# Edge layers of a graph network: TensorE's part of the running maxima ahead of the sum by node

## The chip, the cores and the metric

One core of one Trainium2 chip runs the kernel. The metric is the device time of one execution in microseconds; it is the median of three runs.

## What is computed

The reference is a graph network of four layers on 3,125 nodes with 128 features each and 103,125 edges, sorted by the node that they go to (`dst`). Each layer works on a normalized copy of the features and is added back to them. Layer 0 is a transformer convolution (two heads of 128, with 32 attributes per edge, and a small network behind it), layer 1 three graph attention convolutions in a row (four heads of 64, 64 and 32), layer 2 spline networks and an attention of the second kind (gatv2), layer 3 attention by dot products. Six times in all the same is done by edge; for a graph attention convolution it reads:

```
xp = (x @ W).reshape(n, H, C)
al_src = (xp * a_src).sum(-1)
al_dst = (xp * a_dst).sum(-1)
e = jax.nn.leaky_relu(al_src[s] + al_dst[d], NEG_SLOPE)
m = jax.ops.segment_max(e, d, num_segments=n)
p = jnp.exp(e - m[d])
denom = jax.ops.segment_sum(p, d, num_segments=n)
alpha = p / denom[d]
out = jax.ops.segment_sum(alpha[:, :, None] * xp[s], d, num_segments=n)
```

So each edge layer has a gather of rows by source, a maximum over the edges of each node, and a sum of weighted rows over the edges of each node.

## The kernel before

The function `message_pass` (L394) is called once for each of the six edge layers: kind conv (once), gat (three times), gatv2 and dot. Its edges lie in 427 groups of 256, two tiles of 128 edges each, so that a group's edges all go to nodes of one block of 128. Twelve groups are a chunk (the last three chunks have 7, 6 and 6), which makes 37 chunks. The gathered rows lie in a ring of three chunks. Everything is written out without loops on the chip.

The work goes through the chunks in steps (`steps`): in step i every engine reads chunk i (`expand`), takes the maxima of chunk i-1 (`node_maxima`, in gatv2 `all_maximum`), and sums chunk i-2 (`scatter`), group by group. The engines meet by semaphores:

- POOL (GpSimd) issues two indirect gathers per group (L476) into the ring. From the fourth chunk on it first waits for `scat` of the group three chunks back (L472), since its gathers write over that group's rows.
- PE (TensorE): `expand` (L786) spreads the block's node values to the edges by a matmul with a one-hot matrix (L795 gat, L802 dot and gatv2, L809 conv). `scatter` (L812) adds up the messages of a group by node with two matmuls (L820, x4 in the trace where a product of float32 is two passes) and raises `scat`; it waits for the one-hot matrix, the messages and a free bank. `node_maxima` (L823) makes one link of the maxima's chain in groups 0, 2, 4, 6 and 8: transposes at L833 (group 0), L837 and L838 (group 2), L842 and L843 (group 4), L848 (group 6), and the matmul L852 (group 8). `all_maximum` (L855) has two links, at groups 0 and 2.
- DVE (VectorE) makes the other links in groups 1, 3, 5, 7 and 9, each from what PE's link of the group before left in PSUM (`mx_ps`): scans over the edges L676 and L677; scans over the tiles L682 and L684; L689 to L693; the subtractions L699 to L701; L707 and L708. Beside it DVE weighs the rows of a group (`messages`, L609), adds a group's sums to the nodes' (`add`, L618, two groups behind the scatter), scales the sums of a block that goes on in the next chunk (L633), and in conv computes the logits (L553) and the one-hot matrices.
- ACT (ScalarE) makes one-hot matrices (L893 to L918), conv's messages (L929, which wait for the scatter of the group before), the exponentials (L949, L960) at group 9 and the shrink factor (L969) at group 11.
- SP issues the small loads.

The order of PE's work is that of the function `step` below: in the gat layers a group is scatter, maxima, expand; in the others expand of the next group, scatter, maxima.

Of the kernel before, what the change touches and what calls it, by code (L numbers as in the profile page):

```python
# [39 lines left out]
RING = 3  # L40
# [93 lines left out]
def behind(eng, sem, value):  # L134

    if not (isinstance(value, int) and value <= 0):
        eng.wait_ge(sem, value)
# [256 lines left out]
def message_pass(c, T, name, kind, H, C, W, F, table, nd, acc, attr=None, att=None, ring=None, own_to=None):  # L394
# [68 lines left out]
    with nc.Block() as block:  # L463
# [319 lines left out]
        def _(pe):  # L783
            def expand(i, r, g, use):

                n = BASE[i] + g  # L786
                block_of = pe.value_load(T.blk[0:1, bass.ds(n, 1)], min_val=0, max_val=NB - 1)
                mine = nd[:, bass.ds(block_of, 1), :].rearrange("p o w -> p (o w)")
                pe.wait_ge(s("ohT"), n + 1)
                pe.nop(nofuse=True)  # L790
                if gat:
                    for u in range(2):
                        t = 2 * g + u
                        at = t % 12 * 24
                        last = pe.matmul(ex_ps[:, t // 12, at:at + 24], ohT[:, n % OHB, u, :], mine, start=True, stop=True)  # L795
                    last.then_inc(s("ex"), 1)
                if dot or gatv2:
                    behind(pe, s("prod" if dot else "z"), n - EXB + 1)
                    pe.nop(nofuse=True)
                    width = P if dot else F  # L800
                    for u in range(2):
                        last = pe.matmul(ex_ps[:, n % EXB, u * width:(u + 1) * width], ohT[:, n % OHB, u, :],  # L802
                                         mine[:, 0:width], start=True, stop=True)
                    last.then_inc(s("ex"), 1)
                if conv:
                    for u in range(2):
                        behind(pe, s("logits"), 2 * n - 3 + u)
                        pe.nop(nofuse=True)
                        pe.matmul(ex_ps[:, 2 * (n % 2) + u, 0:F], ohT[:, n % OHB, u, :], mine, start=True, stop=True  # L809
                                  ).then_inc(s("ex"), 1)  # L810

            def scatter(i, r, g):  # L812
                m = BASE[i] + g
                pe.wait_ge(s("oh"), m + 1)
                pe.wait_ge(s("msg"), m + 1)
                pe.wait_ge(s("added"), m + 1)
                pe.nop(nofuse=True)
                for u in range(2):
                    rows = msgs[:, m % 2, u, :] if conv else ring[:, r, 2 * g + u, W - F:W]
                    last = pe.matmul(sc_ps[:, m % SCB, 0:F], oh[:, m % 4, u, :], rows, start=(u == 0), stop=(u == 1))  # L820
                last.then_inc(s("scat"), 1)

            def node_maxima(ch, r, at):  # L823
                if at == 0:
                    if conv:
                        pe.wait_ge(s("logits"), 2 * BASE[ch + 1])
                        if ch >= FULL:
                            pe.wait_ge(s("short"), ch - FULL + 1)
                    else:
                        pe.wait_ge(s("by_v"), ch + 1)  # L830
                    behind(pe, s("shrink_log"), ch)
                    pe.nop(nofuse=True)
                    pe.transpose(mx_ps[0:HT, V_T:V_T + P], lg[:, r if conv else 0, :], T.ident[:]).then_inc(s("v_T"), 1)  # L833
                if at == 2:
                    pe.wait_ge(s("ends"), 2 * ch + 2)
                    pe.nop(nofuse=True)
                    pe.transpose(row_of(0), fwd[:, P - 1:P], T.turn[0:HT, 0:HT])  # L837
                    pe.transpose(row_of(1), bwd[:, 0:1], T.ident[0:HT, 0:HT]).then_inc(s("rows_T"), 1)  # L838
                if at == 4:
                    pe.wait_ge(s("runs"), 2 * ch + 2)  # L840
                    pe.nop(nofuse=True)
                    pe.transpose(mx_ps[0:HT, INTO:INTO + 1], runs[:, 0, 0:HT], T.ident[0:1, 0:1])  # L842
                    pe.transpose(mx_ps[0:HT, INTO + 1:INTO + 2], runs[:, 1, 1:HT + 1], T.ident[0:1, 0:1]  # L843
                                 ).then_inc(s("into_T"), 1)
                if at == 6:
                    pe.wait_ge(s("whole"), ch + 1)
                    pe.nop(nofuse=True)
                    pe.transpose(mx_ps[:, WHOLE:WHOLE + HT], whole[:], T.ident[0:HT, 0:HT]).then_inc(s("whole_T"), 1)  # L848
                if at == 8:
                    pe.wait_ge(s("delta"), ch + 1)  # L850
                    pe.nop(nofuse=True)
                    pe.matmul(mx_ps[:, DELTA:DELTA + H], T.ones[:], delta[:], start=True, stop=True  # L852
                              ).then_inc(s("delta_all"), 1)

            def all_maximum(ch, at):  # L855
                if at == 0:
                    pe.wait_ge(s("by_v"), ch + 1)
                    pe.nop(nofuse=True)
                    pe.transpose(mx_ps[0:1, 0:P], top1[:], T.ident[:]).then_inc(s("v_T"), 1)
                if at == 2:  # L860
                    pe.wait_ge(s("delta"), ch + 1)
                    pe.nop(nofuse=True)
                    pe.matmul(mx_ps[:, P:P + 2], T.ones[:], delta[:], start=True, stop=True).then_inc(s("delta_all"), 1)

            def step(i, r, use, reads, maxima, sums_, before):
                read = SIZES[i] if reads else 0
                summed = SIZES[i - 2] if sums_ else 0
                if reads and not gat:
                    expand(i, r, 0, use)
                for g in range(GC):  # L870
                    if not gat and g + 1 < read:
                        expand(i, r, g + 1, use)
                    if g < summed:
                        scatter(i - 2, (r + 1) % RING, g)
                    if maxima:
                        if gatv2:
                            all_maximum(i - 1, g)
                        else:
                            node_maxima(i - 1, (r - 1) % RING, g)
                    if gat and g < read:  # L880
                        expand(i, r, g, use)

            steps(pe, step)

        @block.scalar
# [1165 lines left out]
```

## Time and profile before

| | |
|---|---|
| Median of 3 runs | 9,028.36 us (9,025.22 to 9,031.15) |
| The profiled execution | 9,009.74 us, span 9,007.9 |
| Busy share of the span | ScalarE 59%, TensorE matmuls 57%, GpSimd 57%, VectorE 51% |
| Granted TensorE clock, mean | 0.707 of full speed |
| Share of the 16 DMA engines | software queue 22.8%, hardware queue 8.1% |

The profile takes one execution. A group's idle time is what its engine stood before it, with the engine whose signal ended the wait; "issue" is time in which it waited for nothing that the profile shows, and "remote" is a signal without a sender in the trace. Where an engine that has long been done is named (a transfer of the first layer in a later one), the length is right and the name is not.

### The profile page before, as it was taken

Reading aid. Unit: us, or ns where it says so; the run is one execution under the profiler, and the core shown is the slowest. Engines: PE = TensorE matmul, PEld = TensorE weight load, DVE = VectorE, ACT = ScalarE, POOL = GpSimd, SP = SyncE. Lnnn points to the kernel's source line nnn. Section 1 sums busy time; section 2 is a strip of 40 time slices with the busy share of each in tenths; the row PEclk is TensorE's granted clock in tenths of the full one; section 3 lists DMA queues with packets and bytes.
Section 4 is the critical chain, followed back from the end, with each engine's and each line's share of the span. In section 5 each row is a group of like instructions: output and inputs, shape, how many; then the busy total and the mean of one; then the engine's idle time right before and its main releaser. Section 6 shows DMA issues by size and latency. Waiting matters only on the chain. (4 is left out here: it accounts for less than half of the span.)

```text
span 9007.9 us, 129245 instructions
## 1 busy us (share of the span) xinstructions
PE 5135.4 (57%) x21094; PEld 3892.3 (43%) x21094; DVE 4622.3 (51%) x15579; ACT 5326.5 (59%) x14791; POOL 5155.8 (57%) x5195
## 2 busy tenths in 40 slices
PE   4778877445555635555534444444565564566666
PEld 2444444334334424344423334433555553455555
DVE  3666666435444524444533333364565565455555
ACT  1777776256666546666636666663566664566665
POOL 3555553266666456666556666635666663566664
PEclk7999999667777767776755555566766766666666
DMA  2222221134434234444322222201222222333332
GB/s 67 72 74 74 71 74 51 52 105 112 110 111 111 86 110 111 113 111 112 102 70 69 70 68 70 66 15 47 67 66 66 66 66 67 97 107 108 108 110 78
DMA packets 428332, 744.58 MB, mean 83 GB/s; under 512 B 207788, under 2 KB 248113, under 8 KB 427439
## 3 DMA queue, kind: packets, MB, share of 16 engines
q0 software_dynamic: 205312, 519.10, 22.8%
q1 hardware_dynamic: 218976, 215.57, 8.1%
q8 instruction: 246, 4.03, 0.2%
q14 instruction: 518, 4.24, 0.2%
q10 hardware_dynamic: 3280, 1.64, 0.1%
HBM read 718.36 MB, written 17.56 MB: 82 GB/s over the span
## 5 line engine op out<-in xcount | busy, mean ns | idle before, releaser
L476 POOL DMA_INDIRECT gat_ring<-tab,gat_ixb x2562 | 2535.1, 989 | 1478.1 <-issue 792.4
L820 PE MATMUL gat_sc_ps<-gat_ring,gat_oh 128*128 128x264 f32 (+1 forms) x5124 | 1892.5, 517 | 1554.3 <-issue 775.4
L820 PEld LDWEIGHTS gat_sc_ps<-gat_ring,gat_oh 128*128 128x128 f32 x5124 | 1208.5, 281 | 1729.3 <-issue 1601.2
L912 ACT ACTIVATE gat_ohT<-gat_offT,one 128x256 bf16<-128x256 bf16 x1281 | 637.9, 498 | 1122.1 <-issue 935.6
L476 POOL DMA_INDIRECT conv_ring<-tab,conv_ixb x854 | 811.9, 951 | 674.0 <-issue 310.3
L476 POOL DMA_INDIRECT dot_ring<-tab,dot_ixb x854 | 833.3, 976 | 624.7 <-issue 306.8
L476 POOL DMA_INDIRECT gatv_ring<-tab,gatv_ixb x854 | 835.2, 978 | 517.7 <-issue 267.1
L898 ACT ACTIVATE gat_off<-iota,rel 128x128 bf16<-128x128 f32 x2562 | 867.9, 386 | 0.1
L618 DVE TENSOR_TENSOR acc<-acc,gat_sc_ps 128x264 f32 (+1 forms) x1281 | 486.6, 380 | 595.6 <-remote 297.3
L809 PE MATMUL conv_ex_ps<-nd,conv_ohT 128*128 x1708 | 602.8, 477 | 324.5 <-issue 111.7
L609 DVE TENSOR_TENSOR gat_ring<-gat_ring,gat_p_sb 128x520 f32<-128x520 f32 (+1 forms) x1281 | 767.2, 599 | 4.1
L929 ACT ACTIVATE conv_msgs<-conv_ring,conv_p_sb 128x161 f32<-128x161 f32 x1708 | 589.2, 416 | 287.7 <-remote 132.6
L820 PE MATMUL dot_sc_ps<-dot_ring,dot_oh 128*128 128x132 f32 x1708 | 446.2, 409 | 433.3 <-issue 371.7
L820 PE MATMUL gatv_sc_ps<-gatv_ring,gatv_oh 128*128 128x132 f32 x1708 | 416.8, 388 | 446.7 <-issue 317.8
L918 ACT ACTIVATE gat_oh<-gat_off,one 128x256 f32<-128x256 bf16 x1281 | 631.8, 493 | 32.4 <-PE gat_sc_ps L820 9.1
L893 ACT ACTIVATE gat_offT<-gat_rel_row,pid 128x256 bf16<-128x256 bf16 x1281 | 631.6, 493 | 8.3 <-DMA gat_rel_row<-d_rel 8.2
L553 DVE SCALAR_TENSOR_TENSOR conv_junk<-conv_ring,conv_ex_ps 128x161 f32<-128x161 f32 x1708 | 453.6, 317 | 344.5 <-PE conv_ex_ps L809 199.1
L820 PEld LDWEIGHTS dot_sc_ps<-dot_ring,dot_oh 128*128 128x128 f32 x1708 | 365.2, 295 | 486.1 <-issue 485.1
L820 PE MATMUL conv_sc_ps<-conv_msgs,conv_oh 128*128 128x322 f32 x1708 | 554.6, 450 | 16.9 <-issue 9.6
L820 PEld LDWEIGHTS gatv_sc_ps<-gatv_ring,gatv_oh 128*128 128x128 f32 x1708 | 342.8, 279 | 498.7 <-issue 495.3
L795 PEld LDWEIGHTS gat_ex_ps<-nd,gat_ohT 128*128 128x128 bf16 x2562 | 281.2, 123 | 641.1 <-issue 559.6
L809 PEld LDWEIGHTS conv_ex_ps<-nd,conv_ohT 128*128 128x128 f32 x1708 | 305.6, 198 | 543.7 <-issue 473.5
(455 smaller groups left out, 10073.3 us busy)
## 6 DMA issues: line engine op xcount, KB each, us to landing
gat_rel_row<-d_rel SPq DMA_DIRECT2D x216, 384.0 KB
gat_ring<-tab,gat_ixb POOLq DMA_INDIRECT x2562
conv_rel_row<-d_rel SPq DMA_DIRECT2D x72, 384.0 KB
gatv_rel_row<-d_rel SPq DMA_DIRECT2D x72, 384.0 KB
dot_rel_row<-d_rel SPq DMA_DIRECT2D x72, 384.0 KB
conv_ring<-tab,conv_ixb POOLq DMA_INDIRECT x854
conv_ring<-in_attr SPq DMA_DIRECT2D x427, 32.0 KB
gatv_ring<-tab,gatv_ixb POOLq DMA_INDIRECT x854
```

Of the source, the lines that this page charges most:

```text
L476: gp.indirect_dma_start(out=ring[:, r, t, 0:width], out_offset=None, in_=table[:, :], in_offset=bass.IndirectOffsetOnAxis(ap=ixb[:, r, t:t ...
L553: last = v.scalar_tensor_tensor(junk[:, u, h, :], ring[:, r, t, :], 1.0, ex_ps[:, 2 * (n % 2) + u, h * W:(h + 1) * W], ALU.mult, ALU.mult, ...
L609: v.tensor_tensor(val, val, bcast(w, [P, 2, H, C + 1], 3), ALU.mult).then_inc(s("msg"), 1)
L618: v.tensor_tensor(here, here, sc_ps[:, m % SCB, 0:F], ALU.add).then_inc(s("added"), 1)
L795: last = pe.matmul(ex_ps[:, t // 12, at:at + 24], ohT[:, n % OHB, u, :], mine, start=True, stop=True)
L809: pe.matmul(ex_ps[:, 2 * (n % 2) + u, 0:F], ohT[:, n % OHB, u, :], mine, start=True, stop=True).then_inc(s("ex"), 1)
L820: last = pe.matmul(sc_ps[:, m % SCB, 0:F], oh[:, m % 4, u, :], rows, start=(u == 0), stop=(u == 1))
L893: a.activation(offT[:, n % 2, :], rel_row[:, n // RG % RB, n % RG, :], ACT.Abs, bias=T.pid[:], scale=-1.0).then_inc(s("offT"), 1)
L898: last = a.activation(off[:, m % 2, u, :], T.iota[:], ACT.Abs, bias=T.rel[:, bass.ds(m * 2 + u, 1)], scale=-1.0)
L912: a.activation(ohT[:, n % OHB].rearrange("p u e -> p (u e)"), offT[:, n % 2, :], ACT.Relu, bias=T.one[:], scale=-1.0).then_inc(s("ohT"), 1)
L918: a.activation(oh[:, m % 4], off[:, m % 2], ACT.Relu, bias=T.one[:], scale=-1.0).then_inc(s("oh"), 1)
L929: last = a.activation(msgs[:, m % 2, u, h * W:(h + 1) * W], ring[:, r, t, :], ACT.Copy, scale=p_sb[:, r, h * ROW + t:h * ROW + t + 1])
```

## The change

In `step` of TensorE's program the block with the maxima is put ahead of the scatter of the same group, for all six edge layers.

```
@@ -870,13 +870,13 @@
                 for g in range(GC):
                     if not gat and g + 1 < read:
                         expand(i, r, g + 1, use)
-                    if g < summed:
-                        scatter(i - 2, (r + 1) % RING, g)
                     if maxima:
                         if gatv2:
                             all_maximum(i - 1, g)
                         else:
                             node_maxima(i - 1, (r - 1) % RING, g)
+                    if g < summed:
+                        scatter(i - 2, (r + 1) % RING, g)
                     if gat and g < read:
                         expand(i, r, g, use)
```

The instructions are the same ones, and the lists of VectorE, ScalarE, GpSimd and SyncE are unchanged. On TensorE, at group 6 of a chunk of a gat layer (`gat_ex_ps` is the expand's result, `gat_sc_ps` the scatter's, `gat_mx_ps` the maxima's), the list before is:

```order
L795 MATMUL gat_ex_ps<-nd,gat_ohT 128x24 x2
L820 MATMUL gat_sc_ps<-gat_ring,gat_oh 128x264 x2
L848 MATMUL gat_mx_ps<-ident,gat_whole 128x104
L787 TENSOR_LOAD blk
L787 ISA x2
L795 ISA
L795 MATMUL gat_ex_ps<-nd,gat_ohT 128x24 x2
```

And now:

```order
L795 MATMUL gat_ex_ps<-nd,gat_ohT 128x24 x2
L848 MATMUL gat_mx_ps<-ident,gat_whole 128x104
L820 MATMUL gat_sc_ps<-gat_ring,gat_oh 128x264 x2
L787 TENSOR_LOAD blk
L787 ISA x2
L795 ISA
L795 MATMUL gat_ex_ps<-nd,gat_ohT 128x24 x2
```

The transpose L848 has taken the scatter's place, and the expand of the group is still the last. The other four places of a chunk move alike.

In conv at group 2 TensorE's list before is (`conv_fwd` and `conv_bwd` are VectorE's two scans of the group before):

```order
L809 MATMUL conv_ex_ps<-nd,conv_ohT 128x322 x2
L820 MATMUL conv_sc_ps<-conv_msgs,conv_oh 128x322 x2
L837 MATMUL conv_mx_ps<-turn,conv_fwd 1x52
L838 MATMUL conv_mx_ps<-ident,conv_bwd 1x52
L787 TENSOR_LOAD blk
```

And now:

```order
L809 MATMUL conv_ex_ps<-nd,conv_ohT 128x322 x2
L837 MATMUL conv_mx_ps<-turn,conv_fwd 1x52
L838 MATMUL conv_mx_ps<-ident,conv_bwd 1x52
L820 MATMUL conv_sc_ps<-conv_msgs,conv_oh 128x322 x2
L787 TENSOR_LOAD blk
```

The expand of the next group stays ahead of both; the scatter now stands behind the wait for the two scans.

## Rows read from the trace of the kernel before

**Rows 1.** The page: busy time by engine
```profile
PE 5135.4 (57%) x21094; PEld 3892.3 (43%) x21094; DVE 4622.3 (51%) x15579; ACT 5326.5 (59%) x14791; POOL 5155.8 (57%) x5195
```

**Rows 2.** Stretches: us, busy PE, PEld, DVE, ACT, POOL, PEclk, DMA share, GB/s
```profile
200.00:1560.00 1360.00, 1085.63 (x3668) 655.77 (x3668) 925.19 (x5101) 976.82 (x2720) 743.93 (x782) 0.96 0.28 69
1760.00:3100.00 1340.00, 723.22 (x2828) 513.57 (x2829) 630.69 (x1562) 815.77 (x2326) 844.90 (x842) 0.71 0.39 109
3170.00:4480.00 1310.00, 708.08 (x2740) 501.70 (x2740) 601.40 (x1478) 796.73 (x2271) 852.40 (x852) 0.70 0.40 110
4550.00:5900.00 1350.00, 598.19 (x2951) 520.00 (x2951) 486.86 (x1577) 824.08 (x2373) 826.61 (x855) 0.52 0.27 68
6230.00:7520.00 1290.00, 772.74 (x3475) 662.78 (x3475) 778.94 (x2475) 790.17 (x2214) 770.54 (x786) 0.71 0.26 63
7680.00:8990.00 1310.00, 817.80 (x3656) 707.92 (x3656) 696.28 (x2207) 805.96 (x2287) 767.90 (x785) 0.67 0.37 101
```

**Rows 3.** Groups by line, shapes apart: out<-in xcount | busy, mean ns | idle before
```profile
L676 DVE TENSOR_TENSOR_SCAN gat_fwd<-gat_pen,gat_mx_ps 104x128 f32<-104x128 f32 x111 | 46.7, 421 | 97.1 <-PE gat_mx_ps L833 65.8 <-issue 28.8 <-remote 2.3
...
L682 DVE TENSOR_TENSOR_SCAN gat_runs<-gat_passes,gat_mx_ps 1x104 f32<-1x104 f32 x111 | 39.5, 356 | 317.8 <-DMA conv_ring<-in_attr 127.2 <-remote 115.7 <-issue 58.7
...
L689 DVE COPY gat_into<-gat_mx_ps 104x2 f32<-104x2 f32 x111 | 17.7, 159 | 205.3 <-PE gat_mx_ps L843 93.2 <-remote 68.4 <-DMA conv_ring<-in_attr 27.3
...
L699 DVE TENSOR_TENSOR gat_low_own<-gat_own,gat_mx_ps 128x104 f32<-128x104 f32 x111 | 29.1, 262 | 130.2 <-issue 60.6 <-PE gat_mx_ps L848 38.8 <-remote 29.2
...
L707 DVE COPY gat_lg<-gat_runs 1x4 f32<-1x4 f32 x111 | 18.3, 165 | 559.1 <-remote 312.8 <-DMA conv_ring<-in_attr 175.6 <-PE gat_mx_ps L852 42.7
```

**Rows 4.** Tile gat_mx_ps: who waited for what it holds (us, times)
```profile
  DVE gat_fwd L676: 65.8, 68
...
  DVE gat_runs L682: 8.0, 14
```

**Rows 5.** Order in time, 2500 to 2545: start, us, engine, line [idle before]
```profile
2507.06 2.10 PE L820 MATMUL gat_sc_ps<-gat_ring,gat_oh 128*128 128x264 f32 x4 [10.40 <-issue]
...
2508.95 0.42 PE L833 MATMUL gat_mx_ps<-ident,gat_lg 128*104 128x128 f32 x1
...
2509.51 0.42 DVE L676 TENSOR_TENSOR_SCAN gat_fwd<-gat_pen,gat_mx_ps 104x128 f32<-104x128 f32 x1 [1.22 <-PE gat_mx_ps L833]
...
2513.35 1.14 PE L820 MATMUL gat_sc_ps<-gat_ring,gat_oh 128*128 128x264 f32 x4
```

**Rows 6.** Order in time, 3683 to 3707
```profile
3691.06 0.38 PE L852 MATMUL gat_mx_ps<-gat_delta,ones 1*128 1x4 f32 x2
...
3699.94 0.94 POOL L476 DMA_INDIRECT gat_ring<-tab,gat_ixb  x1 [0.30 <-issue]
...
3701.56 0.16 DVE L707 COPY gat_lg<-gat_runs 1x4 f32<-1x4 f32 x1 [10.28 <-DMA conv_ring<-in_attr]
...
3702.55 2.10 PE L820 MATMUL gat_sc_ps<-gat_ring,gat_oh 128*128 128x264 f32 x4 [9.94 <-issue]
...
3703.77 0.94 POOL L476 DMA_INDIRECT gat_ring<-tab,gat_ixb  x1 [2.89 <-DMA conv_ring<-in_attr]
```

**Rows 7.** Waits of POOL, 1760 to 5900: us in total, times, longest
```profile
POOL gat_ring L476 <- remote: 193.4, 71, 3.5
...
POOL gat_ring L476 <- PE gat_sc_ps L820: 148.5, 177, 20.6
...
POOL gat_ring L476 <- DMA conv_ring<-in_attr: 138.3, 58, 3.4
...
POOL gat_ring L476 <- DMA pen<-d_pen: 114.6, 56, 3.3
```

**Rows 8.** Groups by line, shapes apart, of conv and dot
```profile
L553 DVE SCALAR_TENSOR_TENSOR conv_junk<-conv_ring,conv_ex_ps 128x161 f32<-128x161 f32 x1708 | 453.6, 317 | 344.5 <-PE conv_ex_ps L809 199.1 <-remote 99.0 <-issue 36.4
...
L676 DVE TENSOR_TENSOR_SCAN conv_fwd<-conv_pen,conv_mx_ps 52x128 f32<-52x128 f32 x37 | 15.1, 409 | 20.0 <-remote 16.6 <-issue 2.1 <-PE conv_mx_ps L833 1.3
...
L676 DVE TENSOR_TENSOR_SCAN dot_fwd<-dot_pen,dot_mx_ps 104x128 f32<-104x128 f32 x37 | 15.4, 417 | 43.2 <-remote 41.6 <-PE dot_mx_ps L833 1.3 <-issue 0.2
```

More of the change, by code:

```diff
@@ L872, in step @@
                         expand(i, r, g + 1, use)
-                    if g < summed:
-                        scatter(i - 2, (r + 1) % RING, g)
                     if maxima:
@@ L879, in step @@
                             node_maxima(i - 1, (r - 1) % RING, g)
+                    if g < summed:
+                        scatter(i - 2, (r + 1) % RING, g)
                     if gat and g < read:
```

## The prediction

> **What bounds the kernel now.** I read the page first, then a table of stretches (one for each of the six edge layers), then the grouped lines of VectorE (DVE), and last the order in time of a few bursts. [rows 1] say that no engine is near full: ScalarE 59%, TensorE (PE) and GpSimd (POOL) 57%, VectorE 51%. [rows 2] take the six layers in turn: conv, three gat layers, gatv2, dot, about 1,330 us each. In the gat layers VectorE is busy for 487 to 631 us of 1,310 to 1,350, TensorE's matmuls for 598 to 723, and GpSimd, which issues the gathers, for 827 to 852.
>
> GpSimd is the pace of the gat layers. A gather takes 0.94 us and the next follows after 0.30 [rows 6], so the 24 gathers of a chunk (12 groups of two) take 24 x 1.25 = 30 us. One gat layer is 37 chunks, 111 over the three. [rows 7] list what else GpSimd stood for in them: 193.4 + 148.5 + 138.3 + 114.6 = 594.8 us, 5.4 us a chunk. 30 + 5.4 = 35.4 is nearly the whole period of a chunk (the three stretches of [rows 2] are 4,000 us, 36.0 a chunk). Each such pause is a wait for a free slot: a gather into the ring waits until the sum by node (the `scat` count of TensorE) of the group three chunks back is done. So what the time depends on is how soon TensorE's scatters come.
>
> They come in bursts. [rows 6] are one. At 3691.06 TensorE does the last matmul of the maxima (0.38 us), which VectorE's L707 only waits for; but L707 starts at 3701.56, 10.28 us later, 0.7 us after GpSimd's gather of 3699.94 has ended and nothing more is issued. Then all move: scatter at 3702.55 after 9.94 us idle, and GpSimd goes on at 3703.77 after 2.89. The scatter of [rows 5] at 2507.06 also stands behind 10.40 idle us. I read this so: while GpSimd issues without a pause, TensorE's work is seen late by others; after GpSimd stops, some groups are worked off fast. The long pauses of [rows 7] (71 + 58 + 56 = 185, of 2.0 to 2.7 us each on average) are 1.7 a chunk, about seven groups each. That it is GpSimd's issuing that delays the others is my reading of the coincidence, not proven by it.
>
> The engine named beside such a stretch ("DMA conv_ring<-in_attr" in a gat layer, "remote") has long been done, so the name is worth nothing and the length is all.
>
> Of these the Trainium skill (Perfetto Trace Analysis, section "Per-instruction lifecycle") says that a matmul's end in a profile is computed from its size, and that its semaphore update comes after that end. L707's 10.28 us agree in kind; a tail of that length no sentence there gives.
>
> **The change, part by part.** No instruction is added or taken away. Within a group TensorE's list loses one place of order: the maxima's transpose or matmul (groups 0, 2, 4, 6, 8 of a chunk; 0 and 2 in gatv2) stands ahead of the group's scatter. VectorE's, ScalarE's, GpSimd's and SyncE's lists are the same. What is behind the moved wait is the scatter of the same group and, in the gat layers, the expand.
>
> A, the gat layers. VectorE does its next part of the maxima one group later and used to wait for TensorE's transpose, since a scatter stood before it. [rows 5] show it: scatter at 2507.06 for 2.10 us, transpose L833 at 2508.95, VectorE's scan at 2509.51 after 1.22 us idle. With the transpose first it starts some 2 us earlier and the scan finds it done. The ordinary waits of this kind, by name, are 65.8 (L676), 93.2 (L689), 38.8 (L699), 42.7 (L707) and 8.0 (L682) [rows 3, 4]: 248.5 us over 111 chunks, 2.24 a chunk. A scatter takes 2.10 us, or 1.14 at the higher clock [rows 5], and the mean of such a wait (65.8 / 68 = 0.97 us at L676 [rows 4]) is shorter than what is moved out of its way, so they go whole.
>
> That is VectorE's time and not the kernel's. It counts inside a burst: 2.24 / 1.7 = 1.3 us of one of 9 to 10 us, some 14% of it. Where VectorE paces the burst, GpSimd gets more slots for each pause; where TensorE's own scatters do (2.10 us for a group of two gathers, 2.5 us of GpSimd), nothing. I take two thirds, 10% fewer pauses: 0.10 x 594.8 = **-60 us**. Bounds: 0, when the groups per pause stay as they are, and -248.5, when each waiting microsecond is on the path.
>
> B, the same waits in conv, gatv2 and dot. The conv and dot scans at L676 lost 1.3 us each to TensorE [rows 8]; five such lines by three layers at that size are 20 us, half of them on the path: **-10 us** (bounds 0 and -20). The long ones in dot (41.6 of its 43.2) are of the kind of [rows 6] and are not touched.
>
> C, a new wait in conv. There TensorE at group 2 wants VectorE's two scans of the maxima, 0.41 us and about as much, and only then does the scatter. VectorE does them after its own work of the group before, so the scatter may stand: 0.8 us x 5 places x 37 chunks = 148 us if all of it is exposed. I cost it at **0**, since TensorE is not what ends last: VectorE waits 199.1 us for the expand L809 [rows 8], and the expand still goes ahead of both moved items, as in the row order of the change; behind the scatter stands only the next expand, which wants VectorE's logits of the same group anyway. If that cover is gone, the price is 148. The messages of ScalarE, which wait for scatters, are behind it too.
>
> Sum: -60 - 10 + 0 = -70 against the profiled execution's 9,009.7: 8,939.7. The median of the runs is 9,028.4, 18.6 above it, and I forecast on the median's basis: **8,958**.
>
> **The rivals.**
> R1, no difference. Bursts end where they end now, since what opens them is GpSimd's stop; each pause lets through a whole number of groups, and 1.3 us do not make one more. For it: the pauses' mean length, 2.0 to 2.7 us, is nearly one size. Against it: pauses by "PE gat_sc_ps L820" have a spread of sizes (177 of them, 148.5 us). 9,028.
>
> R2, slower. At the groups where a burst runs dry, TensorE now stands at the maxima's wait with the scatter behind it, where it used to give the slot free first. Before, a late sight of VectorE's part (groups 2 and 8 most, where [rows 6] and L682's 317.8 us stand) cost nothing as long as the scatter was ahead. Its price by the nearest row is the moved work and its handshake: 0.42 us for the transpose [rows 5] and about 0.1 around it, at two places in 111 chunks: 0.5 x 2 x 111 = 111 us, +111: 9,139. It decides once GpSimd's pause ends with the scatter of such a group; below that it is hidden. If instead every wait were a whole scatter late (2.10), it would be 466 us; I take no such case as likely, as VectorE's part stands one group ahead. For conv the same sign comes from term C, 148.
>
> R3, the long waits shorten too. L682 has 317.8 idle us and L707 559.1 [rows 3], together 876.9, most of it the long kind. If the matmuls for L682 and L707 are among those seen before GpSimd's stretch begins, since they stand 1 to 2 us earlier, a third goes: 292 us, 8,736. For it: the matmul of [rows 6] missed by less than that. Against: one wait moved out of a stretch is replaced by the next thing that waits in it.
>
> R4, the clock. The granted clock is 0.71, 0.70 and 0.52 in the gat layers [rows 2], and a scatter takes 2.10 us at the lower level (1.2 GHz), 1.14 at the higher (2.4 GHz) [rows 5]. A burst that starts a long idle time later starts at the lower. If the order filled the bursts so that the third layer came to 0.70, the share of 0.36 (0.18 / 0.5) of 427 groups would be 0.97 us shorter each: 149 us at most, 8,879. Against it: the same work in the same bursts gives the same gaps. The Trainium skill (TensorE: Matmul & The Clock Gate, section "Why this matters for your kernels") has idle gaps between bursts of matmuls as what brings the lower clock; by that rule the change helps only if it closes gaps, and the rows' 9.94 us of idle are not closed by it.
>
> **How the numbers follow.** My forecast (pauses fall by a tenth, -20 to -150 us) has 0.36; R1 0.22; R2, with C, 0.26; R3 0.12; R4 0.04. Sign: faster by more than 0.2% (18 us, about what a measurement of this kernel can tell from no change) is 0.36 + 0.12 + 0.04 = 0.52, the same 0.22, slower 0.26. The likeliest is the forecast, 8,958. Its own range is 8,878 to 9,010. The range of 8 in 10 takes in R1 and R4 and the most of R2: 8,850 to 9,150. It leaves out R3 (0.12) and some 0.06 of R2's end, where both places and conv's add.
>
> **What would show it.** In the profile after: the idle before L676, L689 and L699 named after TensorE near zero (from 65.8, 93.2, 38.8); GpSimd's pauses in the gat layers down from 595 to about 535, fewer rather than shorter; the issue order scatter behind L833, L838, L848, L852. R1: the waits at L676 and L689 gone, pauses and time as before, the idle moved to L618 or L654. R2: pauses of GpSimd named after `gat_sc_ps` longer, or in conv more idle before L820 and L929. R3: L682 and L707 together far below 877. R4: a granted clock above 0.6 in the third gat layer. I am wrong in the base if the pauses of GpSimd change by an amount that the span doesn't follow.

## The result, and the profile after

The changed kernel takes 8,997.2 us (median of 14 runs, 8,968.9 to 9,022.0) against 9,024.4 (14 runs, 9,012.0 to 9,043.9): ratio 0.9969, 95% interval 0.9961 to 0.9977. It is faster by 27 us (21 to 35 by the interval of the ratio). The forecast was -70. All differences in us, here and below, are differences of the two medians; the ratios have their own estimate and can differ from them by some us.

The profiled execution after took 9,018.7 us, which is 21.5 above its kernel's median, while the one of before was below its own. So the two profiles can't be subtracted as totals; what they show is where each engine stands. The page after, busy time by engine (against [rows 1]):

```profile
PE 5067.1 (56%) x21094; PEld 3795.5 (42%) x21094; DVE 4587.0 (51%) x15579; ACT 5324.4 (59%) x14791; POOL 5189.0 (58%) x5195
```

TensorE's matmuls and VectorE are busy for 68 and 35 us less, GpSimd for 33 us more. Nothing is near full, as before.

VectorE's lines in the gat layers after, grouped by line (the columns are those of [rows 3]), with GpSimd's gathers:

```profile
L476 POOL DMA_INDIRECT gat_ring<-tab,gat_ixb x2562 | 2562.4, 1000 | 1458.2 <-issue 785.9 <-PE gat_sc_ps L820 239.0 <-DMA pen<-d_pen 122.2
...
L618 DVE TENSOR_TENSOR acc<-acc,gat_sc_ps 128x264 f32 x854 | 362.9, 425 | 740.5 <-DMA pen<-d_pen 239.1 <-PE gat_sc_ps L820 234.9 <-DMA conv_ring<-in_attr 192.4
...
L654 DVE TENSOR_REDUCE gat_ex_sum<-gat_ex_ps 128x192 f32<-128x576 f32 x102 | 77.1, 756 | 422.8 <-issue 145.9 <-DMA conv_ring<-in_attr 142.9 <-remote 94.1
...
L676 DVE TENSOR_TENSOR_SCAN gat_fwd<-gat_pen,gat_mx_ps 104x128 f32<-104x128 f32 x111 | 45.8, 412 | 2.3 <-PE gat_mx_ps L833 1.4 <-issue 0.9
...
L682 DVE TENSOR_TENSOR_SCAN gat_runs<-gat_passes,gat_mx_ps 1x104 f32<-1x104 f32 x111 | 39.4, 355 | 220.4 <-remote 104.4 <-issue 82.6 <-DMA conv_ring<-in_attr 32.0
...
L699 DVE TENSOR_TENSOR gat_low_own<-gat_own,gat_mx_ps 128x104 f32<-128x104 f32 x111 | 28.3, 255 | 50.2 <-issue 28.4 <-PE gat_mx_ps L848 17.5 <-remote 2.8
...
L707 DVE COPY gat_lg<-gat_runs 1x4 f32<-1x4 f32 x111 | 18.9, 170 | 344.3 <-remote 185.6 <-issue 77.7 <-PE gat_mx_ps L852 49.7
...
L689 DVE COPY gat_into<-gat_mx_ps 104x2 f32<-104x2 f32 x111 | 17.0, 153 | 96.0 <-PE gat_mx_ps L843 28.3 <-remote 26.1 <-DMA conv_ring<-in_attr 22.3
```

Three of these lines before, which stand in no group ahead:

```profile
L476 POOL DMA_INDIRECT gat_ring<-tab,gat_ixb x2562 | 2535.1, 989 | 1478.1 <-issue 792.4 <-remote 193.4 <-PE gat_sc_ps L820 148.5
...
L618 DVE TENSOR_TENSOR acc<-acc,gat_sc_ps 128x264 f32 x854 | 360.5, 422 | 170.0 <-PE gat_sc_ps L820 71.6 <-issue 30.3 <-DMA conv_ring<-in_attr 29.1
...
L654 DVE TENSOR_REDUCE gat_ex_sum<-gat_ex_ps 128x192 f32<-128x576 f32 x102 | 77.2, 757 | 352.1 <-issue 254.0 <-PE gat_ex_ps L795 55.7 <-remote 42.5
```

The waits that the change aimed at shrank, but only one line's are gone: L676 went from 97.1 idle us to 2.3, L689 from 205.3 to 96.0, L699 from 130.2 to 50.2. By TensorE's name, where the prediction had 248.5 us that "go whole", 98.1 are left: 1.4 (L676), 28.3 (L689), 17.5 (L699), 1.2 (L682) and 49.7 (L707, before 42.7). Even the long ones shrank, L682 from 317.8 to 220.4 and L707 from 559.1 to 344.3: together the five lines of [rows 3] lost 596 us. But the line of the sums, L618, took up 170.0 to 740.5, and L654 352.1 to 422.8, together 641. VectorE waits as long as before, at another line. And a row that nobody waits at has moved: a gather of GpSimd lasts 1,000 ns on average, not 989, 27 us in 2,562.

GpSimd's waits in the gat layers, after (against [rows 7]):

```profile
POOL gat_ring L476 <- PE gat_sc_ps L820: 239.0, 196, 20.6
POOL gat_ring L476 <- DMA pen<-d_pen: 122.2, 53, 3.5
POOL gat_ring L476 <- remote: 115.8, 43, 3.4
POOL gat_ring L476 <- DMA conv_ring<-in_attr: 104.2, 48, 3.4
```

Their sum is 581.2 us, before 594.8: 14 us less, where the forecast had 60. All idle time before L476, whatever its name, fell by 20 (1,478.1 to 1,458.2 in the lines above), and the gathers' own 27 us more use that up. The pauses without the scatter's name are fewer (144 in place of 185) and those with it longer, but that is mostly a matter of names: of all pauses between two gathers of a gat layer, 205 last 1.5 to 5 us before and 199 after.

### The profile page after: what moved, and what is told of

Its sections match the earlier page's. It is cut to its first block and busy times, and to the rows that moved or that the text cites. A ratio compares the mean times of both kernels' runs of the same rounds, so it can differ in the third digit from the quotient of the medians.

```text
span 9016.2 us, 129245 instructions
## 1 busy us (share of the span) xinstructions
PE 5067.1 (56%) x21094; PEld 3795.5 (42%) x21094; DVE 4587.0 (51%) x15579; ACT 5324.4 (59%) x14791; POOL 5189.0 (58%) x5195
## 5 line engine op out<-in xcount | busy, mean ns | idle before, releaser
L476 POOL DMA_INDIRECT gat_ring<-tab,gat_ixb x2562 | 2562.4, 1000 | 1458.2 <-issue 785.9
L820 PE MATMUL gat_sc_ps<-gat_ring,gat_oh 128*128 128x264 f32 (+1 forms) x5124 | 1788.6, 502 | 605.4 <-issue 307.7
L820 PEld LDWEIGHTS gat_sc_ps<-gat_ring,gat_oh 128*128 128x128 f32 x5124 | 1176.3, 274 | 803.4 <-issue 673.9
L476 POOL DMA_INDIRECT conv_ring<-tab,conv_ixb x854 | 812.5, 951 | 685.1 <-issue 317.3
L476 POOL DMA_INDIRECT dot_ring<-tab,dot_ixb x854 | 837.7, 981 | 627.6 <-issue 270.2
L476 POOL DMA_INDIRECT gatv_ring<-tab,gatv_ixb x854 | 835.9, 979 | 517.1 <-issue 273.5
L618 DVE TENSOR_TENSOR acc<-acc,gat_sc_ps 128x264 f32 (+1 forms) x1281 | 489.2, 382 | 1143.9 <-PE gat_sc_ps L820 354.7
L809 PE MATMUL conv_ex_ps<-nd,conv_ohT 128*128 x1708 | 595.8, 472 | 328.2 <-ACT conv_ohT L912 120.4
L609 DVE TENSOR_TENSOR gat_ring<-gat_ring,gat_p_sb 128x520 f32<-128x520 f32 (+1 forms) x1281 | 768.2, 600 | 4.1
L929 ACT ACTIVATE conv_msgs<-conv_ring,conv_p_sb 128x161 f32<-128x161 f32 x1708 | 589.3, 416 | 281.8 <-PE conv_sc_ps L820 127.4
L553 DVE SCALAR_TENSOR_TENSOR conv_junk<-conv_ring,conv_ex_ps 128x161 f32<-128x161 f32 x1708 | 453.3, 317 | 410.1 <-PE conv_ex_ps L809 255.3
L820 PE MATMUL dot_sc_ps<-dot_ring,dot_oh 128*128 128x132 f32 x1708 | 416.9, 387 | 433.6 <-issue 281.7
L795 PE MATMUL gat_ex_ps<-nd,gat_ohT 128*128 x2562 | 291.5, 190 | 551.2 <-issue 506.8
L809 PEld LDWEIGHTS conv_ex_ps<-nd,conv_ohT 128*128 128x128 f32 x1708 | 307.7, 197 | 591.5 <-issue 517.9
```

Source lines behind the costliest of these rows:

```text
L476: gp.indirect_dma_start(out=ring[:, r, t, 0:width], out_offset=None, in_=table[:, :], in_offset=bass.IndirectOffsetOnAxis(ap=ixb[:, r, t:t ...
L553: last = v.scalar_tensor_tensor(junk[:, u, h, :], ring[:, r, t, :], 1.0, ex_ps[:, 2 * (n % 2) + u, h * W:(h + 1) * W], ALU.mult, ALU.mult, ...
L609: v.tensor_tensor(val, val, bcast(w, [P, 2, H, C + 1], 3), ALU.mult).then_inc(s("msg"), 1)
L618: v.tensor_tensor(here, here, sc_ps[:, m % SCB, 0:F], ALU.add).then_inc(s("added"), 1)
L929: last = a.activation(msgs[:, m % 2, u, h * W:(h + 1) * W], ring[:, r, t, :], ACT.Copy, scale=p_sb[:, r, h * ROW + t:h * ROW + t + 1])
```

## The experiments

The runs fell on four chips, and these are of two kinds. On chip 1 the kernel before takes 8,917 us and has the pauses and late signals of [rows 6, 7]. On chips 2, 3 and 4 the same kernel takes 7,522 to 7,525 us: GpSimd's gathers follow one another after 0.3 us throughout a gat layer there. In r1, the kernel before on chip 3, the waits by name are:

```profile
POOL gat_ring L476 <- issue: 742.2, 2436, 0.3
...
POOL gat_ring L476 <- PE gat_sc_ps L820: 37.2, 122, 0.3
```

The only longer ones stand where a layer starts. What makes the two kinds differ was not looked for: it may be the chip or something around it, and "kind of chip" is only a name for what was seen. All ratios are to the kernel before on the same chip. The result above is of a chip of the first kind (9,024 us).

### Chip 1: which layers, and what a wait of VectorE costs

The edit of e1, e2 and e3 keeps both orders in `step` and chooses by the layer's kind; e6 puts four of the five links later instead of earlier:

```
+                    first = gat        # e2: conv   e3: dot or gatv2
+                    if g < summed and not first:
                         scatter(i - 2, (r + 1) % RING, g)
...
+                    if g < summed and first:
+                        scatter(i - 2, (r + 1) % RING, g)
# e6, gat layers:
                     if g < summed:
                         scatter(i - 2, (r + 1) % RING, g)
+                    if maxima and gat and (g == 0 or g in (3, 5, 7, 9)):
+                        node_maxima(i - 1, (r - 1) % RING, g - 1 if g else 0)
...
```

> The new order in the three gat layers only. If the change acts through GpSimd's pauses there (594.8 us before, 581.2 after), it gives about -14 us: ratio 0.998. If VectorE's idle time before its maxima lines is on the path (1,310 us before, 713 after), far more than the whole change gave: below 0.98. If the gain came from elsewhere: 1.000.

Measured: 0.9974 (0.9964 to 0.9983), -22 us.

> The new order in conv only. If term C is hidden, as predicted (0): ratio 1.000. If the scatter behind the two scans is exposed there: up to +148 us, 1.016. VectorE's idle time before L553 rose in the profile after from 344.5 to 410.1 us, 66 us, which would be 1.007 if it is on the path.

Measured: 1.0014 (1.0004 to 1.0023), +10 us.

> The new order in dot and gatv2 only. By the prediction's term B about -7 us of its -10: 0.999. If the long waits gone from L676 of dot (43.2 to 0.2) and L726 of gatv2 (61.7 to 0.0) were on the path: -105 us, 0.988. If they have only moved to other lines: 1.000.

Measured: 0.9997 (0.9988 to 1.0006), -5 us. The 105 us of idle time that left L676 of dot and L726 of gatv2 were not on the path.

> The suspected cost doubled: in the gat layers the maxima's links of groups 2, 4, 6 and 8 stand behind the scatter of the NEXT group, so VectorE waits for a whole scatter (1.13 to 2.10 us) at 4 places in 111 chunks, 444 in all. If such waits are on the path: +500 to +900 us, 1.06 to 1.10. If they only take up time in which VectorE would stand for GpSimd's pauses anyway: within +60 us, up to 1.007.

Measured: 1.0156 (1.0142 to 1.0171), +145 us, or 0.33 us for each of the 444 links that wait for a scatter of 1.13 to 2.10 us. Between the two expectations: such a wait reaches the end with a part of it.

The three parts sum to -16 us, with the intervals' width about as large; the whole had -27, where the kernel before took 9,024 us. The gain lies in the gat layers, and conv gives some back. GpSimd's waits in the gat layers of e1:

```profile
POOL gat_ring L476 <- remote: 153.1, 68, 3.2
POOL gat_ring L476 <- PE gat_sc_ps L820: 139.7, 156, 3.1
POOL gat_ring L476 <- DMA conv_ring<-in_attr: 105.3, 54, 3.5
POOL gat_ring L476 <- DMA pen<-d_pen: 103.7, 50, 3.1
```

And of e6:

```profile
POOL gat_ring L476 <- PE gat_sc_ps L820: 358.9, 277, 16.2
POOL gat_ring L476 <- remote: 179.8, 71, 3.4
...
POOL gat_ring L476 <- DMA pen<-d_pen: 82.8, 43, 2.9
POOL gat_ring L476 <- DMA conv_ring<-in_attr: 78.6, 42, 2.9
```

They sum to 501.8 and 700.1 us. In e2 and e3, whose gat layers have the order of before on the same chip, the same four rows sum to 530.5 and 545.8, mean 538. So by these names the pauses moved by -36 in e1 and by +162 in e6. But the names don't hold all of it: "issue" has part of the pauses too. The gathers' whole line, of e1, e2, e3 and e6 in this order:

```profile
L476 POOL DMA_INDIRECT gat_ring<-tab,gat_ixb x2562 | 2557.1, 998 | 1420.2 <-issue 827.2 <-remote 153.1 <-PE gat_sc_ps L820 139.7
...
L476 POOL DMA_INDIRECT gat_ring<-tab,gat_ixb x2562 | 2548.7, 995 | 1422.0 <-issue 800.3 <-remote 182.7 <-PE gat_sc_ps L820 151.3
...
L476 POOL DMA_INDIRECT gat_ring<-tab,gat_ixb x2562 | 2555.9, 998 | 1421.4 <-issue 784.2 <-remote 182.2 <-PE gat_sc_ps L820 180.9
...
L476 POOL DMA_INDIRECT gat_ring<-tab,gat_ixb x2562 | 2505.9, 978 | 1585.5 <-issue 794.5 <-PE gat_sc_ps L820 358.9 <-remote 179.8
```

In e6 all idle time before the gathers rose by 164 us over the mean of e2 and e3, and the gathers themselves took 46 less: +118 of the +145. So on this kind of chip GpSimd's pauses carry most of what a wait added to VectorE costs. In e1 the idle time is that of e2 and e3 (1,420.2 against 1,422.0 and 1,421.4): the pauses did not fall, their names changed. Where e1's 22 us lie is not shown by these profiles, one of each kernel, in which e1's execution (8,901.1 us) is only 6 us shorter than e3's (8,906.8).

### Chips 2 to 4: the same change is slower

Two runs that were to tell groups 0, 4, 6 from 2 and 8 came out on chip 2 beside two with half of the gathers left out:

```
+                    first = gat and g in (0, 4, 6)        # e4, r3
+                    first = gat and g in (2, 8)           # e5, r4
# e7 (order of before), e8 (new order):
-                    for u in range(2):
+                    for u in range(2 if ch < RING else 1):
```

> In the gat layers, the new order only in groups 0, 4 and 6 of a chunk, whose links carry 197.8 of the 248.5 us of waits by TensorE's name (L676, L689, L699). If the gain goes by these ordinary waits: four fifths of the gat gain of 0.9974, so 0.998. If it comes from groups 2 and 8, where the long waits stand (L682 and L707, 877 us before, 565 after): 1.000.

Measured: 1.0121 (1.0106 to 1.0137).

> The complement: in the gat layers the new order only in groups 2 and 8 (waits by TensorE's name 50.7 us of 248.5). If the gain goes by the ordinary waits: 0.9995. If by the long ones at L682 and L707: 0.9975. By rival R2 (the scatter that frees GpSimd's slot stands one place later there): slower, up to 1.012.

Measured: 1.0165 (1.0151 to 1.0179). Both expectations were for the other kind of chip; neither half gains here.

> The order of before, but from the fourth chunk on GpSimd gathers only the first of a group's two tiles (the second tile's rows are those of an earlier chunk), 2,562 + 216 gathers in place of 5,124. If GpSimd's 24 x 1.25 us a chunk is the pace of the edge layers, the time falls by far: each gat chunk from 36 us to what VectorE and TensorE need, 20 to 28, ratio 0.70 to 0.85. If the chain between VectorE and TensorE is the pace: above 0.95.

Measured: 0.8482 (0.8470 to 0.8494), at the slow end of the first range. GpSimd is the pace of the kernel before on this chip; the edit halves the transfers with the gathers, but the gaps of 0.3 us alone say the same.

> The same half of the gathers left out, with the new order. If VectorE's waits for TensorE (248.5 us in the gat layers) were only covered by GpSimd's pace, they are on the path here and the new order gives more than it gave in full: 100 to 250 us less than e7. If TensorE's scatters are the pace then, both are alike within 0.3%; if conv's term C (148 us) comes onto the path, e8 is slower than e7.

Measured: 0.8509 (0.8497 to 0.8521), 21 us behind e7. From the first gather of the first gat layer to the first of gatv2, e8 is 13 us shorter (2,926 against 2,939), where 100 to 250 were expected if the waits were on the path; something in conv costs more than that. But the test says less than it was meant to, since with half of the gathers another engine sets the pace. A stretch of e7's second gat layer (columns as in [rows 2]):

```profile
2430.00:3250.00 820.00, 573.86 (x2771) 418.39 (x2772) 608.87 (x1513) 774.74 (x2277) 468.71 (x448) 0.87 0.38 108
```

ScalarE is busy for 774.74 of 820 us, 94%, against VectorE's 608.87. None of the expectations had that.

Then the kernel before and the changed one were run with a profile on chip 3, beside e4 and e5 again:

> The kernel before, unchanged, for a profile on the same chip as the next three. Ratio 1.000 within 0.1%. On a chip of the kind where GpSimd never stands in the gat layers (before 7,523 us) its gathers in the gat layers should be shorter than the 1,015 and 1,025 ns on average that e4 and e5 had, if the +1.2% and +1.65% of those lie in them: 92 us / 2,562 = 36 ns less. On a chip of the other kind (9,000 us) they take 989 to 1,000 ns and GpSimd's pauses are 530 to 595 us.

Measured: 1.0000 (0.9991 to 1.0009).

> The changed kernel on the same chip. Where before takes 9,000 us: 0.997. Where before takes 7,523 us: slower, 1.01 to 1.02, if what e4 and e5 showed adds up; with GpSimd's gathers longer and no pause at all.

Measured: 1.0187 (1.0173 to 1.0200), +141 us: the change that gains 0.3% on one kind of chip loses 1.9% on the other.

> As e4 (gat layers, groups 0, 4 and 6 alone), beside r2 on the same chip. Where before takes 9,000 us: 0.998 if the gain goes by the ordinary waits, 1.000 if by groups 2 and 8. Where it takes 7,523: 1.012 again.

Measured: 1.0130 (1.0115 to 1.0146), +98 us.

> As e5 (gat layers, groups 2 and 8 alone), beside r2 on the same chip. Where before takes 9,000 us: 0.9995 if the gain goes by the ordinary waits, 0.9975 if by the long ones, above 1.002 by rival R2. Where it takes 7,523: 1.0165 again.

Measured: 1.0166 (1.0152 to 1.0180), +126 us. Which groups carry the gain on chip 1 stays open.

Groups by line of r1, the kernel before on chip 3:

```profile
L476 POOL DMA_INDIRECT gat_ring<-tab,gat_ixb x2562 | 2492.7, 973 | 870.1 <-issue 742.2 <-ACT gat_ixb L934 90.7 <-PE gat_sc_ps L820 37.2
...
L929 ACT ACTIVATE conv_msgs<-conv_ring,conv_p_sb 128x161 f32<-128x161 f32 x1708 | 589.7, 417 | 106.6 <-PE conv_sc_ps L820 96.6
...
L609 DVE TENSOR_TENSOR gat_ring<-gat_ring,gat_p_sb 128x520 f32<-128x520 f32 x854 | 586.6, 687 | 2.6
...
L553 DVE SCALAR_TENSOR_TENSOR conv_junk<-conv_ring,conv_ex_ps 128x161 f32<-128x161 f32 x1708 | 447.2, 317 | 133.9 <-PE conv_ex_ps L809 95.6 <-DMA conv_ring<-tab,conv_ixb 32.9 <-DVE conv_junk L553 0.8
...
L654 DVE TENSOR_REDUCE gat_ex_sum<-gat_ex_ps 128x192 f32<-128x576 f32 x102 | 77.3, 757 | 1190.8 <-SPq L485 1190.8
...
L707 DVE COPY gat_lg<-gat_runs 1x4 f32<-1x4 f32 x111 | 21.4, 193 | 57.1 <-PE gat_mx_ps L852 56.9
```

And of r2, the changed one:

```profile
L476 POOL DMA_INDIRECT gat_ring<-tab,gat_ixb x2562 | 2601.1, 1015 | 870.7 <-issue 731.3 <-ACT gat_ixb L934 99.6 <-PE gat_sc_ps L820 39.9
...
L929 ACT ACTIVATE conv_msgs<-conv_ring,conv_p_sb 128x161 f32<-128x161 f32 x1708 | 589.1, 416 | 158.1 <-PE conv_sc_ps L820 157.5
...
L553 DVE SCALAR_TENSOR_TENSOR conv_junk<-conv_ring,conv_ex_ps 128x161 f32<-128x161 f32 x1708 | 447.2, 318 | 195.7 <-PE conv_ex_ps L809 161.4 <-DMA conv_ring<-tab,conv_ixb 29.8 <-DVE conv_junk L553 0.6
...
L654 DVE TENSOR_REDUCE gat_ex_sum<-gat_ex_ps 128x192 f32<-128x576 f32 x102 | 77.3, 758 | 1545.5 <-SPq L485 1545.5
...
L707 DVE COPY gat_lg<-gat_runs 1x4 f32<-1x4 f32 x111 | 22.8, 206 | 9.7 <-PE gat_mx_ps L852 9.7
```

Here no late signal spoils the picture: L707 stood 57.1 us before, nearly all by TensorE's name, and 9.7 after. What the time follows is the first row: the same 2,562 gathers are busy for 2,492.7 us and then for 2,601.1, +108.4. Some 100 of them lie in the first two gat layers, where the weighing L609 takes 0.69 us, and 8 in the third, where it takes 0.42. VectorE meanwhile waits longer at L654 for the gathered chunk (1,190.8, then 1,545.5). A piece of r4 in order of time shows what lengthens one gather:

```profile
2020.58 2.78 POOL L476 DMA_INDIRECT gat_ring<-tab,gat_ixb  x1 [0.30 <-PE gat_sc_ps L820]
2020.64 0.33 DVE L684 TENSOR_TENSOR_SCAN gat_runs<-gat_passes,gat_mx_ps 1x104 f32<-1x104 f32 x1
...
2020.90 0.66 DVE L609 TENSOR_TENSOR gat_ring<-gat_ring,gat_p_sb 128x520 f32<-128x520 f32 x1
...
2021.49 0.41 DVE L618 TENSOR_TENSOR acc<-acc,gat_sc_ps 128x264 f32 x1
...
2021.83 0.68 DVE L609 TENSOR_TENSOR gat_ring<-gat_ring,gat_p_sb 128x520 f32<-128x520 f32 x1
...
2022.44 0.41 DVE L618 TENSOR_TENSOR acc<-acc,gat_sc_ps 128x264 f32 x1
...
2023.09 0.16 DVE L689 COPY gat_into<-gat_mx_ps 104x2 f32<-104x2 f32 x1 [0.24 <-PE gat_mx_ps L843]
```

A gather that else takes 0.95 us takes 2.78. From its start to 2022.85 VectorE runs one instruction into the next; then it is idle for 0.24 us, and the gather ends at 2023.36, 0.51 us after that run. The weighing of the rows, L609, reads two operands from SBUF. In r2 all 313 gathers above 1.1 us in the first two gat layers lie over an L609 (25% of the shorter ones do); in r1 there are 131, all over an L609 too (38% of the shorter ones). Call this the collision theory: a gather that meets VectorE's dense work waits for it, and the waits of VectorE that the change removed were the gaps in which GpSimd got on with its gather. The other, the chain theory, has the loss in the order of the waits between TensorE and VectorE, however long L609 is.

One thing speaks against a simple count of gaps. The five lines of [rows 3] have 259 idle us in r1, 25 in r2, 133 in r3 and 178 in r4. So r4 takes the least from VectorE and lengthens the gathers the most (2,630.2 us, +138), and r3 and r4, which share the five groups between them, have +104 and +138 where both together have +108. It seems to count where VectorE's work comes to lie over the gathers; no run tells what decides that.

It was tested on chip 2 by shortening L609 and by cutting it in two:

```
# r5, r6: one head of four is weighed in the gat layers
+                    v.tensor_tensor(val[:, :, 0:1], val[:, :, 0:1], bcast(w[:, :, 0:1], [P, 2, 1, C + 1], 3), ALU.mult
# r7, r8, v1, v2: one instruction per tile, the same work
+                    for u in range(2):
+                        last = v.tensor_tensor(val[:, u], val[:, u], bcast(w[:, u], [P, H, C + 1], 2), ALU.mult)
```

> Order of before; in the gat layers VectorE's L609 weighs only one head of four (the other three are summed unweighted), so that it takes some 0.2 us in place of 0.69. Collision theory: the gathers of the gat layers fall towards 0.95 us each, 2,562 x 0.95 = 2,434 us (from 2,493 on a chip of the 7,525 kind, from 2,535 on one of the 9,000 kind). Chain theory: they stay as they are.

Measured: 0.9941 (0.9927 to 0.9955), -50 us.

> The same with the new order. Collision theory: gathers 2,434 us here too, so that on a 7,525 chip r6 is behind r5 by conv's share alone (45 us, 0.6%) in place of 141 us; on a 9,000 chip the new order gains more than 28 us over r5. Chain theory: r6 behind r5 by 1.9% still on a 7,525 chip.

Measured: 0.9983 (0.9974 to 0.9992), 37 us behind r5, where conv's share of 45 was expected and 141 by the chain theory. The gathers of r5:

```profile
L476 POOL DMA_INDIRECT gat_ring<-tab,gat_ixb x2562 | 2442.0, 953 | 870.8 <-issue 720.0 <-ACT gat_ixb L938 91.0 <-PE gat_sc_ps L824 59.7
```

Beside them r5's shortened weighing (its line is L610 there), and then the gathers of r6:

```profile
L610 DVE TENSOR_TENSOR gat_ring<-gat_ring,gat_p_sb 128x130 f32<-128x130 f32 x854 | 243.1, 285 | 2.6
...
L476 POOL DMA_INDIRECT gat_ring<-tab,gat_ixb x2562 | 2444.9, 954 | 870.8 <-issue 712.7 <-ACT gat_ixb L938 91.1 <-PE gat_sc_ps L824 67.0
```

2,442.0 and 2,444.9 us: with L609 at 285 ns in place of 687 the order of TensorE's list makes no difference to the gathers. The loss in the gathers hangs on the length of L609, as the collision theory has it, and the chain theory falls for them. A shorter L609 also makes VectorE's work less dense, so these runs don't say whether it is L609's two operands in SBUF or the unbroken work as such that holds a gather.

> Order of before; in the gat layers L609 is two instructions, one per tile, with the same work. Collision theory: a gather that meets it waits at most half as long, so the excess over 0.95 us (59 us in 2,562 gathers on a 7,525 chip, 101 on a 9,000 chip) falls to a half: ratio 0.995 to 0.998. If the two stand back to back and GpSimd gets in only behind both: 1.000. VectorE has 1,190 us of idle time at L654 on the 7,525 kind, so the added fixed cost is hidden there; on the 9,000 kind it may cost up to 427 x 3 x 0.1 = 128 us of VectorE's bursts.

Measured: 0.9989 (0.9980 to 0.9998).

> The same cut with the new order. Collision theory: on a 7,525 chip half of the 108 us comes back, ratio 1.010 to 1.014 against 1.0187 whole; on a 9,000 chip at or below 0.997. Chain theory: as r2, 1.0187, or 0.997.

Measured: 1.0099 (1.0084 to 1.0115): nearly half of the loss comes back.

> New order in the gat layers alone, conv, gatv2 and dot as before, L609 cut in two. On a 9,000 chip: e1's 0.9974 less what the cut saves of the gathers' excess over 0.95 us (some 120 us in 2,562 gathers, half of it 60): 0.991 to 0.995; if VectorE's added fixed cost counts in the bursts, 0.998 to 1.005. On a 7,525 chip: r8 less conv's 45 us, 1.004.

Measured: 1.0032 (1.0020 to 1.0045), on chip 4.

> The order of before with L609 cut in two. On a 7,525 chip 0.9989 again. On a 9,000 chip 0.995 if half of the excess of the gathers (101 us) comes back, 1.000 to 1.005 if VectorE's added fixed cost counts in the bursts.

Measured: 0.9986 (0.9977 to 0.9995), on chip 4. The cut in the order of before is the only one of these edits that does the whole work and beats the kernel before on this kind of chip, by 0.11 and 0.14%; how it does on the other kind wasn't seen.

All changed runs with every gather on chips 2 to 4 (us; gathers are the busy time of L476 in the gat layers less r1's 2,492.7; conv's part is the time from the start of its first gather to that of its last, 1,135 us in r1 and 1,180 in r2, r6 and r8):

| run | gathers | conv | sum | time measured |
|---|---|---|---|---|
| r2, the change | +108 | +45 | +153 | +141 |
| r3, groups 0, 4, 6 | +104 | 0 | +104 | +98 |
| r4, groups 2, 8 | +138 | 0 | +138 | +126 |
| r5, short L609, before | -51 | 0 | -51 | -50 |
| r6, short L609, after | -48 | +45 | -3 | -13 |
| r7, cut, before | -22 | 0 | -22 | -11 |
| r8, cut, after | +38 | +45 | +83 | +70 |
| v1, cut, gat layers | +39 | 0 | +39 | +29 |
| v2, cut, before again | -20 | 0 | -20 | -9 |

Two terms give every one of nine times within 13 us. Both are read from the same runs' profiles, so they say where the time lies; that L609 is behind the first is shown by r5 and r6 alone.

### Conv

The 45 us are there with half of the gathers too (conv's stretch is 1,132 us in e7 and 1,178 in e8), so the number of GpSimd's gathers has no part in them. But TensorE doesn't wait for the scans either: its waits before conv's maxima for VectorE are 1.0 us in r1 and 1.9 in r2. In the groups by line of r1 and r2 the idle time of ScalarE's messages L929 behind the scatter goes from 96.6 to 157.5 us and VectorE's L553 behind the expand from 95.6 to 161.4. ScalarE also makes the one-hot matrix that the expand wants (TensorE's L809 waits for it 55.1 us in r1, 80.1 in r2). That chain, scatter later by a transpose, messages, one-hot matrix, expand, logits, is read from these rows; no run took one link of it out.

## Why the prediction was wrong

**What bounds the kernel: right in the main.** GpSimd's gathers and its pauses are the pace: leaving out half of the gathers takes 15% off the time (e7, chip 2), and on chip 1 GpSimd's pauses carry most of what e6's added waits cost. "TensorE's work is seen late by others" while GpSimd issues: [rows 6] show it on that kind of chip; on the other kind, where GpSimd issues without any pause, L707's 111 waits for TensorE sum to 57.1 us in r1. So GpSimd's issuing alone is not its cause. What is stays open.

**Term A, -60: the sign held on chip 1, the size failed.** e1 gives -22. The step that failed is "GpSimd gets more slots for each pause ... I take two thirds, 10% fewer pauses". GpSimd's idle time before its gathers fell by 20 of 1,478 us between the two main profiles and not at all in e1 (1,420.2 against 1,422.0 and 1,421.4), and the freed time stayed with VectorE at L618 (170.0 to 740.5). The step before it, that the 248.5 us go whole, failed too: 98.1 were left, though on chip 3, without the late signals, nearly all went (248.7 to 23.9 by TensorE's name in r1 and r2). Why the pauses hold their length on chip 1, and where e1's 22 us come from, stays open. The sign itself was partly luck: nothing in the prediction tells the one kind of chip from the other, on which the same term is a loss.

**The step that was missing: what VectorE's waits were good for.** The prediction costed a gather at 0.94 us flat and took GpSimd's busy time as given. But [rows 2] had it all along: 842 instructions of GpSimd and 844.90 us, 852 and 852.40, where 0.95 each would be 800 and 809. A gather over L609 can wait, and the waits that the change removes from VectorE were gaps for it. On chip 1 that took 27 us between the two profiles (2,535.1 to 2,562.4); by e1 against e2 and e3 on one chip (2,557 against 2,549 and 2,556) only 1 to 8, so there it is small. The same link shows on chip 1 from the other side: e6, which gives VectorE more waits, has the shortest gathers of that chip, 2,505.9 us. On chips 2 to 4 there are no pauses to win, and it costs 108 of the change's 141 us.

The Trainium skill (SBUF — State Buffer, the section on who interferes with whom) says that VectorE and GpSimd share one pair of ports, and that an instruction of VectorE with two inputs in SBUF contends with a GpSimd instruction that reads SBUF; it adds that `tensor_tensor` was not seen to stall the issuing of transfers. The first agrees with r5 and r6, though no run here shows that it is the ports; against the second stand the 2.78 us of the gather above, whose indices lie in SBUF.

**Term B, -10:** e3 has -5, and its interval takes in no change at all. The term's "five such lines by three layers" counts too many, since gatv2 has two links.

**Term C, 0:** +10 on chip 1 and +45 on the other kind. "Behind the scatter stands only the next expand" left out what the prediction itself named a sentence later, ScalarE's messages. The full 148 of its bound did not come on either.

**The rivals.** R1 (no change) was near for conv, gatv2 and dot. R2 (slower, GpSimd's slot one place late) names the sign of chips 2 to 4 but not the mechanism: GpSimd's waits for the gat scatters there are 37.2 us in r1 and 39.9 in r2. Its sign on chip 1 did show (waits named after the scatter, 148.5 to 239.0), but the total of the pauses didn't grow. R3 had the long waits go from 877 to far below, and they did (565), and it was worth nothing, as its own "against" said: the next thing waits in their place. R4: the third gat layer's granted clock is 0.53 after, 0.52 before ([rows 2]), and the first two have 0.68 after, 0.71 and 0.70 before: the clock gave nothing.

## What to carry to other kernels

In this kernel idle time of VectorE was what GpSimd's gathers lived on: before packing VectorE's work tighter, see whether GpSimd's instructions last longer where they lie over it, and count their busy time as something that the change can move. When waits by one name vanish, add up the engine's idle time over all its lines before booking a gain. And a gain of a few tenths of a per cent on one chip can be a loss of two per cent on another, as here: run both kernels on more than one.

## What the runs showed of the hardware

The same kernel takes 8,917 or 9,024 us on some chips and 7,522 to 7,525 on others, with the same instructions and close busy times (9,008 and 7,519 us of span: VectorE 4,622 and 4,639, ScalarE 5,327 and 5,301, GpSimd 5,156 and 5,087, TensorE's matmuls 5,135 and 4,757 at a granted clock of 0.707 and 0.757). Most of the difference is in the waits between engines: L707 has 559.1 idle us in the one and 57.1 in the other.

A gather that meets a dense run of VectorE's instructions was seen to last up to 2.78 us in place of 0.95. With the weighing L609 at 285 ns in place of 687, 2,562 gathers take 2,444.9 us in place of 2,601.1 in the new order, and 2,442.0 in place of 2,492.7 in the order of before.
